# A scan with a mixture-of-experts FFN behind it: FFN work handed over into the next block, and the clip moved to the front of a step

## What is computed

```python
def _derivative(q, p, drive, coupling, bias):
    i_couple = jnp.tanh(q) @ coupling.T
    dq = q - q ** 3 / 3.0 - p + drive + i_couple + bias
    dp = EPSILON * (q + ALPHA - BETA * p)
    return (dq, dp)
# one step of time: four evaluations of it (Runge-Kutta), then
q_next = jnp.clip(q_next, -CLAMP, CLAMP); p_next = jnp.clip(p_next, -CLAMP, CLAMP)
...
# the FFN, on all 2048 states q
logits = x @ W_router.T
rw, sel = jax.lax.top_k(softmax(logits), 2);  combine[token, sel] = rw
shared_out = (silu_and_mul(x @ Ws_gate_up) @ Ws_down) * sigmoid(x @ W_sgate.T)
gu = jnp.einsum('th,ehi->eti', x, We_gate_up);  h = silu_and_mul(gu)
sparse_out = jnp.einsum('eth,te->th', jnp.einsum('eti,eih->eth', h, We_down), combine)
return shared_out + sparse_out
```

## Time and profile before

| | us |
|---|---|
| median of 3 runs | 743.61 |
| the 3 runs | 742.8, 743.61, 743.67 |
| profiled execution | 745.0 |
| its span, first to last instruction | 743.1 |
| PE, DVE, ACT, POOL busy | 679.2, 671.2, 431.0, 174.6 |

### The profile page before, as it was taken

The page is one execution under the profiler, slowest core; times in us unless marked ns, Lnnn a source line. Parts: engine busy times, 40 slices in busy tenths (PEclk is TensorE's granted clock), DMA queues, the critical chain, the costliest instruction groups (busy, mean ns, idle before and its releaser), DMA issues.

```text
span 743.1 us, 33477 instructions
## 1 busy us (share of the span) xinstructions
PE 679.2 (91%) x12101; PEld 601.7 (81%) x12101; DVE 671.2 (90%) x4624; ACT 431.0 (58%) x2310; POOL 174.6 (23%) x372
## 2 busy tenths in 40 slices
PE   2437999999999999999999999999999999999998
PEld 1326888888888888888888888888888989888888
DVE  5899999999999999999999999999999899999972
ACT  3865646556565655656565565656556565654643
POOL 0001221312222231222223122221312213132233
PEclk9999999999999999999999999999999999999999
DMA  8600000000000000000000000000000000000000
GB/s 319 189 2 2 3 3 11 4 9 4 10 3 3 11 3 10 4 10 4 3 11 3 11 2 11 2 4 10 4 10 4 10 4 2 11 4 10 4 9 9
DMA packets 8630, 13.64 MB, mean 18 GB/s; under 512 B 1520, under 2 KB 7984, under 8 KB 8208
## 3 DMA queue, kind: packets, MB, share of 16 engines
q1 hardware_dynamic: 8464, 11.50, 4.5%
HBM read 9.40 MB, written 2.10 MB: 15 GB/s over the span
## 4 chain that ended last, share of the span: by engine, by line
PE 62%; DVE 22%; issue 7%; ACT 3%; POOL 3%; DMA 2%; SPq 0%; DVEq 0%; POOLq 0%; ACTq 0%
PE up_ps L507 18%; PE down_ps L521 14%; PE coup_ps L456 12%; PE coup_ps L449 11%; PE warm_ps L537 5%; DVE th_lo L685 2%; POOL hidden L839 2%; PE route_ps L488 2%; DMA wf<-in_w_up 2%; DVE q L720 2%; DVE p_part L623 2%; DVE q_raw L720 1%; DVE w L618 1%; DVE p_sum L643 1%; DVE force L707 1%
## 5 line engine op out<-in xcount | busy, mean ns | idle before, releaser
L507 PE MATMUL up_ps<-q_hi,w 128*128 128x128 f16 x2176 | 226.5, 220 | 0.7 <-POOL q_lo L809 0.7
L449 PE MATMUL coup_ps<-th_hi,c 128*128 128x16 f16 x4096 | 183.2, 171 | 30.1 <-ACT th_hi L348 27.8
L449 PEld LDWEIGHTS coup_ps<-th_hi,c 128*128 128x128 f16 x4096 | 148.0, 97 | 71.3 <-ACT th_hi L348 48.0
L348 ACT ACTIVATE th_hi<-q 128x32 f16<-128x32 f32 x384 | 88.0, 229 | 189.0 <-DVE q L720 187.3
L507 PE MATMUL up_ps<-q_lo,w 128*128 128x128 f16 x1088 | 197.2, 220 | 0.0
L839 POOL TENSOR_TENSOR hidden<-hidden,comb_s 128x128 f32<-128x128 f32 x272 | 124.5, 459 | 295.4 <-PE coup_ps L456 274.4
L507 PEld LDWEIGHTS up_ps<-q_hi,w 128*128 128x128 f16 x2176 | 175.0, 98 | 0.8 <-POOL q_lo L809 0.8
L521 PE MATMUL down_ps<-hidden,wd 128*128 128x128 f32 x1088 | 157.8, 285 | 0.0
L456 PE MATMUL coup_ps<-th_lo,c 128*128 128x16 f16 x2048 | 132.2, 173 | 24.3 <-DVE th_lo L685 17.1
L521 PEld LDWEIGHTS down_ps<-hidden,wd 128*128 128x128 f32 x1088 | 133.3, 191 | 0.0
L456 PEld LDWEIGHTS coup_ps<-th_lo,c 128*128 128x128 f16 x2048 | 85.8, 97 | 58.5 <-DVE th_lo L685 32.5
(11 more groups left out here) (87 smaller groups left out, 910.0 us busy)
## 6 DMA issues: line engine op xcount, KB each, us to landing
wf<-in_w_up SPq DMA_DIRECT2D x1, 4224.0 KB, 13.5
wd<-in_w_down SPq DMA_DIRECT2D x1, 2048.0 KB, 22.4
out<-out_s SPq DMA_DIRECT2D x16, 128.0 KB, 2.1
xs<-in_x SPq DMA_DIRECT2D x1, 1920.0 KB, 19.0
sel<-in_spread SPq DMA_DIRECT2D x1, 408.0 KB, 18.8
cf<-in_coupling SPq DMA_DIRECT2D x1, 256.0 KB, 2.4
xs<-in_x SPq DMA_DIRECT2D x1, 128.0 KB, 2.2
ident<-in_identity SPq DMA_DIRECT2D x1, 64.0 KB, 2.3
```

The costliest lines, as they stand in the source:

```text
L348: nc.scalar.activation(th_hi[:], q[:], ACT.Tanh).then_inc(hi_ready, 1)
L449: nc.tensor.matmul(coup_ps[:, m * B:(m + 1) * B], c16[:, part, k, m * P:(m + 1) * P], th_hi[:, k, :], start=part == m == k == 0, stop=Fals ...
L507: last = nc.tensor.matmul(up_ps[j % 4][:, h * TOK:(h + 1) * TOK], w16[:, part, k, h, j * P:(j + 1) * P], q[:, k, :], start=n == 0, stop=n ...
```

## The change

1. **Two blocks of FFN at a time.** The FFN's stages now run from 0 to 43. In stage st of block b the engines do stage st + 32 of block b-2 and stage st of block b-1 (`ffn_stages`). PE takes the newer block first (`[::-1]`), the others the older. The tail is 44 stages long, with the end of block 14 and all of block 15.
2. **New lists.** The hides stand in stages 5, 10, 13 to 31, never where k is 0; a product tile two stages ahead of its hide. Spreads move to 15, 19, 23, 27, 31. Weighs stand in 16 to 30 and 34 to 41, never where k is 3. Eight of 17 down tiles fall into the next block's stages 1 to 10, and PE has no stage any more with two down tiles and a spread.
3. **Router steps one by one.** The seven steps stand in stages 1, 2, 3, 6, 7, 8, 9 instead of two in stage 1 and one each in 2, 4, 5, 6, 7, and share no stage with a hide. The power goes from stage 2 to 3, `comb` from 7, 8, 9 to 10, 11, 12, the turn from 10 to 13.
4. **Final sum.** One instruction of 128x256 in stage 43 (stage 11 of the block two later), instead of two of 128x128 in stages 2 and 3.
5. **`q_lo`** is made in two halves of 128x128, in stages 0 and 1.
6. **The clip first.** Where k is 0, DVE clips q before it makes `rest` for that evaluation, not behind it. The `rest` of the second evaluation goes from the end of the k = 0 stage (behind `force`) to the front of the k = 1 stage, and `base3` and `base4` there go one place back each, behind `cubic` and behind `force`.
7. **Unread matmuls.** `WARM` follows the new lists: 5, 0, 5, 1, 5, 13, 13, 0, 1, 5, 5 in stages 0 to 10 (before: 6, 10, 11, 1, 1, 1, 13, 1, 1, 1, 13), 78 in a block (before: 83).

```diff
-UP_AT = [st for st in range(3, 25) if st % 4 != 2]
-SILU_AT = [s + 1 for s in UP_AT]
-HIDE_AT = [s + 2 for s in UP_AT]
-SPREAD_AT = [12, 15, 18, 22, 26]
+HIDE_AT = [5, 10, 13, 14, 15, 17, 18, 19, 21, 22, 23, 25, 26, 27, 29, 30, 31]
+SILU_AT = [s - 1 for s in HIDE_AT]
+UP_AT = [s - 2 for s in HIDE_AT]
+TURN_AT = 13
+SPREAD_AT = [15, 19, 23, 27, 31]
 COPY_AT = [SPREAD_AT[j // GROUP] + 1 + (j % GROUP) // 2 for j in range(TILES)]
-WEIGH_AT = list(range(13, 30))
-DOWN_AT = [14, 18, 18, 22, 22, 25, 26, 26, 27, 27, 28, 28, 29, 29, 30, 30, 31]
+WEIGH_AT = [16, 17, 18, 20, 21, 22, 24, 25, 26, 28, 29, 30, 34, 37, 38, 40, 41]
+DOWN_AT = [18, 18, 22, 22, 26, 26, 30, 30, 31, 33, 33, 34, 36, 39, 39, 41, 42]
+FINISH_AT = STAGES + 11
 assert len(UP_AT) == len(DOWN_AT) == len(WEIGH_AT) == TILES and len(SPREAD_AT) == GROUPS
 assert all(w >= max(s, c) and d > w for w, s, c, d in zip(WEIGH_AT, HIDE_AT, COPY_AT, DOWN_AT))
-
-WARM = [6, 10, 11] + [max(0, 13 - 12 * UP_AT.count(st) - 8 * DOWN_AT.count(st) - 4 * SPREAD_AT.count(st))
-                      for st in range(3, STAGES)]
+assert DOWN_AT[-1] < FINISH_AT < STAGES + DOWN_AT[0]
+
+WARM = [max(0, 13 - 12 * UP_AT.count(st) - 8 * (DOWN_AT + [0]).count(st) - 8 * DOWN_AT.count(st + STAGES)
+            - 4 * SPREAD_AT.count(st)) for st in range(STAGES)]
...
-ROUTE_AT = {1: (0, 1), 2: (2,), 4: (3,), 5: (4,), 6: (5,), 7: (6,)}
-FINISH_AT = [2, 3]
+ROUTE_AT = {1: (0,), 2: (1,), 3: (2,), 6: (3,), 7: (4,), 8: (5,), 9: (6,)}
...
             for b in range(BLOCKS):
-                block_of(b, b - 1 if b else None)
+                block_of(b)
+
+        def ffn_stages(b, st):
+
+            return [(f, at) for f, at in ((b - 2, st + STAGES), (b - 1, st)) if 0 <= f < BLOCKS]
+
+        def tail_stages():
+
+            return [x for st in range(FINISH_AT + 1) for x in ffn_stages(BLOCKS, st)]
...
-            def one_block(b, f):
+            def one_block(b):
                 for st in range(STAGES):
                     couple(b, st)
                     prepare(b * STAGES + st)
-                    if f is not None:
-                        if isinstance(f, int) and st == 0:
-                            pe.wait_ge(in_wd, 2 * 16)
-                            pe.wait_ge(in_const, 4 * 16)
-                        ffn(f, st)
+                    if b == 1 and st == 0:
+                        pe.wait_ge(in_wd, 2 * 16)
+                        pe.wait_ge(in_const, 4 * 16)
+                    for f, at in ffn_stages(b, st)[::-1]:
+                        ffn(f, at)
+                    if b:
                         for _ in range(WARM[st]):
                             nc.tensor.matmul(warm_ps[:, 0:P], c16[:, 0, 0, 0:P], c16[:, 0, 0, 0:P],
                                              start=True, stop=True)
 
...
 
                     if t:
-                        dve.wait_ge(p_clipped, t)
+                        dve.wait_ge(q_ready, n)
+                        if i == 1 and b:
+                            dve.wait_ge(q_split, (KC + 1) * b)
+                        nc.vector.tensor_scalar(q, q_raw[:], CLAMP, -CLAMP, ALU.min, ALU.max).then_inc(q_clipped, 1)
                     nc.vector.tensor_tensor(rest[0][:], drive[:, t, 0], p_now[:], ALU.subtract
                                             ).then_inc(rest1_ready, 1)
-                    if t:
-                        dve.wait_ge(q_ready, n)
-                        if i == 1 and b:
-                            dve.wait_ge(q_split, 2 * b)
-                        nc.vector.tensor_scalar(q, q_raw[:], CLAMP, -CLAMP, ALU.min, ALU.max).then_inc(q_clipped, 1)
                 prepare(n)
                 slot()
                 if k == 0:
@@ -666,10 +675,10 @@
                 else:
                     dve.wait_ge(q_ready, n)
                 if k == 1:
+
+                    nc.vector.scalar_tensor_tensor(rest[1][:], q0_of(i), R2_Q1, base[:, 0, :].rearrange(
+                        "p (m b) -> p m b", m=KC), ALU.mult, ALU.add).then_inc(rested, 1)
                     update_p()
-
-                    nc.vector.tensor_tensor(base3[:].rearrange("p m b -> p (m b)"), base[:, 1, :],
-                                            q0_of(i), ALU.add).then_inc(based_q, 1)
                 elif k == 2:
 
                     nc.vector.scalar_tensor_tensor(rest[2][:], q_in[1][:], R3_Q2, base3[:], ALU.mult, ALU.add
@@ -691,8 +700,8 @@
                     update_p()
                 elif k == 1:
 
-                    nc.vector.scalar_tensor_tensor(base4[:], q0_of(i), R4_Q1, base[:, 2, :].rearrange(
-                        "p (m b) -> p m b", m=KC), ALU.mult, ALU.add).then_inc(based_q, 1)
+                    nc.vector.tensor_tensor(base3[:].rearrange("p m b -> p (m b)"), base[:, 1, :],
+                                            q0_of(i), ALU.add).then_inc(based_q, 1)
                 elif k == 2:
 
                     nc.vector.scalar_tensor_tensor(base42[:], q_in[1][:], R4_Q2, base4[:], ALU.mult, ALU.add
@@ -705,11 +714,10 @@
 
                 dve.wait_ge(cubed, n + 1)
                 nc.vector.tensor_tensor(force[:], rest[k][:], cubic[:], ALU.subtract).then_inc(forced, 1)
-                if k == 0:
-
-                    dve.wait_ge(based, t + 1)
-                    nc.vector.scalar_tensor_tensor(rest[1][:], q, R2_Q1, base[:, 0, :].rearrange(
-                        "p (m b) -> p m b", m=KC), ALU.mult, ALU.add).then_inc(rested, 1)
+                if k == 1:
+
+                    nc.vector.scalar_tensor_tensor(base4[:], q0_of(i), R4_Q1, base[:, 2, :].rearrange(
+                        "p (m b) -> p m b", m=KC), ALU.mult, ALU.add).then_inc(based_q, 1)
                 elif k == 3 and t + 1 < T:
 
                     dve.wait_ge(p_clipped, t + 1)
@@ -755,16 +763,15 @@
                                                      prob[:, rank:rank + 1], ALU.is_equal, ALU.mult)
                 op.then_inc(routed, 1)
 
-            def finish_chunk(f, m):
-
+            def finish(f):
 
                 dve.wait_ge(down_ready, TILES * (f + 1))
-                if not (isinstance(f, int) and f == 0):
+                if f:
                     dve.wait_ge(stored, 16 * f)
                 nc.vector.tensor_tensor(
-                    out_s[:, m, :].rearrange("p (t b) -> p t b", t=STEPS),
-                    down_ps[:, m * TOK:(m + 1) * TOK].rearrange("p (t b) -> p t b", t=STEPS),
-                    xs[:, bass.ts(f, STEPS), m, :], ALU.add).then_inc(out_ready, 1)
+                    out_s[:].rearrange("p m (t b) -> p m t b", t=STEPS),
+                    down_ps[:, 0:KC * TOK].rearrange("p (m t b) -> p m t b", m=KC, t=STEPS),
+                    xs[:, bass.ts(f, STEPS)].rearrange("p t m b -> p m t b"), ALU.add).then_inc(out_ready, 1)
 
             def ffn(f, st):
                 for r in ROUTE_AT.get(st, ()):
...
-                if f and st in FINISH_AT:
-                    finish_chunk(f - 1, FINISH_AT.index(st))
-
-            def one_block(b, f):
+                if st == FINISH_AT:
+                    finish(f)
...
+                if st < KC:
+
+                    pool.wait_ge(q_split, (KC + 1) * f + 1)
+                    nc.gpsimd.tensor_tensor(q_lo[:, st], q_trace[:, st].rearrange("p t b -> p (t b)"), q_hi[:, st],
                                             ALU.subtract).then_inc(q_split, 1)
-                if st == 2:
```

More of the change, by code:

```diff
@@ L540, in _ @@
             blocks(one_block)
-            for st in range(STAGES):
-                ffn(BLOCKS - 1, st)
+            for f, at in tail_stages():
+                ffn(f, at)
         @block.vector
@@ L780, in ffn, with one_block @@
                                                        ).then_inc(hidden_ready, 1)
[L781 to L784 removed]
+                if st == FINISH_AT:
+                    finish(f)
+            def one_block(b):
                 for st in range(STAGES):
                     def slot(st=st):
[L787 to L788 removed]
+                        for f, at in ffn_stages(b, st):
+                            ffn(f, at)
                     scan_stage(b, st, slot)
@@ L794, in _ @@
                                     ).then_inc(q_clipped, 1)
-            for st in range(STAGES):
-                ffn(BLOCKS - 1, st)
-            for m in range(KC):
-                finish_chunk(BLOCKS - 1, m)
+            for f, at in tail_stages():
+                ffn(f, at)
         @block.gpsimd
```

40 lines of the change are left out of this document (18 added, 22 removed).

## The result

| | before | changed |
|---|---|---|
| median, us | 743.64 (4 runs) | 734.34 (4 runs) |
| runs, us | 742.8 to 743.74 | 733.84 to 735.21 |
| profiled execution; its span | 745.0; 743.1 | 735.21; 733.4 |

The ratio is 0.9879, interval 0.9862 to 0.9896: 9.3 us faster. The forecast was 722.2 with a range from 716 to 731. The sign was right, and more than half of the gain did not come.

What follows compares the result with a forecast made beforehand. The chain tanh, `th_lo`, coupling, next q was taken to bound each stage at 1.29 us. Fourteen blocks -22.8, block 1 -1.1 and tail +2.5 gave -21.4, so 722.2 us, range 716 to 731.

Steps and rivals of the forecast that it cites:

- Lists of weighs and hides: New weigh places: 0.44 us less per block; `p_sum` waiting for a weigh's end, 0.14 into its stage, costs nothing.
- POOL holds first and second: Rival, stage 9: `first` waits for stage 8's weigh, stage grows 0.25 us; 727.8 in all, chance 0.20.
- Block 1: First block with FFN: same relief but no final sum, clock may rise later; 1.1 us less, bounds 0 and 2.
- Clip first: k = 0 stages: `rest` no longer ahead of the clip; 0.04 us less in each of eight, 0.3 per block.
- rival of longer k = 1 stages: Rival: `base4` behind `force` delays L720 by 0.1 us in each k = 1 stage; 735 in all, chance 0.05.
- Down tiles spread out: Stages 19 and 23: no stage with two down tiles and a spread ahead of them; 0.36 us less per block.
- router steps in stages 1 to 7: Router steps alone in their slots: 0.20 us in place of all the excess of stages 1, 4, 5 and 7.
- weighs off `p_part`: Stages 16, 20, 24, 28: no weigh meets the second `p_part`; 0.11 us less each, 0.44 per block.
- Final sum: Stage 11: the single sum waits for the last down passes and adds 0.32 us, bounds 0.2 and 0.45.
- Tail: End of the kernel: more product tiles behind a later turn; 2.5 us more, bounds 1.5 and 4.5.
- Small holds: Anywhere in a block, such as the hold behind a first weigh: 0.1 us allowed per block.

Runs made afterwards that it cites:

- x2_one_wait: Changed kernel, but POOL waits for `coupled` once per stage and only in stages where it has work; 726.15 us.
- x11_q_lo_whole: Kernel of `x2_one_wait` with `q_lo` made by one 128x256 instruction in stage 0, as before the change; 728.41 us.
- x3: Changed kernel with the weigh of tile 15 (stage 8 of the next block) over 8 of its 128 columns; 732.46 us.
- x4: Changed kernel with block 1's unread matmuls filled up for the down tiles that block does not have yet; 733.68 us.
- x9: Changed kernel with one POOL wait for `coupled` per stage, in every stage, also those without work; 727.7 us.

## Why the prediction was wrong, point by point

- *Lists of weighs and hides, "cost nothing; bounds 0 and 0.1".* This step failed. It took a weigh's end, 0.14 into the next stage, from a trace in which POOL had a weigh in every stage from 13 to 29 and passed one `coupled` wait for each, and carried it over to a program that passes two per stage and has stages without a weigh. The diff of POOL's loop shows the added wait; I priced POOL's instructions and not its waits. `x2_one_wait` is 8.2 us faster, and its blocks are 0.57 shorter, 0.57 x 14 = 8.0: stage 17 0.16, stages 21, 25, 29 0.055 each, stage 9 0.23, together 0.56.
- *Rival "POOL holds first and second", 0.25.* It is what happened in stage 9, with 0.23. I gave it 0.20 and took the other value in the sum. That its price came out is luck. It was worked out for a weigh that ends 0.14 into stage 9. In `x2_one_wait` the weigh ends just there (369.39 + 0.46 = 369.85) and `first` keeps its 0.28, which ends at 369.88 anyway: a held row begins on time and ends with the weigh, and does not begin behind it. The 0.23 came because the weigh ended 0.38 into the stage.
- *Block 1, "1.1 less, bounds 0 and 2".* It took 0.47 more: 6.8 us at 1.2 GHz, out of bounds. I had the mechanism and thought of one or two product tiles, and not that the clock, once risen, falls back. Beside stage 9, six stages of the block take 1.7 us: 4, 6 and 7 before the clock rises at 74.2, and 12, 13 and 14 in the stretch shown and at its end. Without that, in `x2_one_wait`'s trace, the block is 1.7 less than before, inside the bounds.
- *Clip first, 0.04 in eight stages.* Right in six. Stages 0 and 8 stay at 1.34. In stage 8 the router's `which_f` now stands in the slot, which I priced at nothing; `th_lo` begins 0.44 into it and 0.38 into stage 12. In stage 0 the clip begins 0.07 into the stage and in stages 8 to 28 0.015, and only there does the vector engine pass a wait of its own for `driven` just ahead of it, so it may be this engine's waits that cost here; that was not tried. The rival of longer k = 1 stages has no part in it: `x2_one_wait` has them at 1.29.
- *Down tiles spread out, 0.36; router steps in stages 1 to 7; weighs off `p_part`, 0.44.* Right: stages 19, 23, 4, 5, 7 and 16, 20, 24, 28 are all at 1.29. Stage 1, forecast at 1.37, is 1.29: the logits' copy begins 0.10 into it and not 0.14, and its 0.08 did not come. `x11_q_lo_whole` shows what else the prediction missed there: with `q_lo` in one piece the stage is 1.42. For stage 9 the forecast had 0.12 for `first` and `second`; with the weighs early it is 0.08.
- *Final sum 0.32.* Measured 0.33, and its length of 0.41 was 0.42. *Tail +2.5.* From the last `th_hi` (715.47 and 703.20 in the two traces) to the span's end it is 27.7 before and 30.2 now, +2.5. The turn of the changed kernel in the chain that ended last, with the last q clipped at 704.49, is 8.2 after it, forecast 8.0:

```profile
704.49 0.19 DVE q_trace L800
...
712.69 0.06 PE route_ps L487
...
726.26 4.09 PE down_ps L531 x36
```

- *Small holds, 0.1.* Too little. Beside what is named above, single stages in single blocks come out 0.07 to 0.35 long: the sum of each stage's median is 42.39, the mean block 42.65, 0.26 more (before 43.51 and 43.56). In block 5's stage 28 the coupling's last pass ends at 273.79 and `force` at 273.82, and the next q begins at 274.26:

```profile
274.26 0.25 DVE L728 SCALAR_TENSOR_TENSOR q<-coup_ps,c_un,force 128x32 f32<-128x32 f32 x1 [0.44 <-DVE force L716]
```

  Nothing that the profile shows held it. It is no accident of one execution: this pause and fourteen more are in the same stages of the same blocks, with lengths within 0.06, in the six kernels with the changed lists and the new order (the changed one, x2, x3, x4, x9, x11), also where earlier stages had become shorter. They go with a place in the vector engine's instruction stream. Counted from the first row of its trace, waits included, the row that comes late is the 64th or 65th of a run of 128 in 12 of the 16 pauses of blocks 2 to 14, which make 3.2 of their 3.7 us (in the trace before 5 of 6, and 0.8 of 0.9 us). The packets of queue q14, which the page calls "instruction", are of 8192 bytes, which is 64 for each of 128. So the fetching of instructions is a suspect; no run tested it, most places 128 rows apart show no pause (12 of 35 do), and the cause stays open. For small differences this matters: a change of order or of lists moves these pauses too, and they differ by 1 to 3 us in all between the traces here.

The terms add up to the miss of a block: late weighs 0.56, stages 0 and 8 0.10, the pauses 0.16 above what I allowed, the sum 0.01, less 0.08 for stage 1 and 0.04 for `first` and `second`, 0.71 of 0.72.

With the POOL waits mended and nothing else, the forecast's own sum would have been 4 us off (726.15), inside its range.

## What to carry to other kernels

A helper loop that now runs twice per step doubles its waits too. Count them as instructions of that engine, above all in front of work whose end some other engine can run into. And when a row's start time is carried over to a new schedule, ask what stands ahead of it in its own queue there: here 0.24 to 0.35 us of lateness on an engine that is busy 24% of the time cost 8 us. The old trace may show the price already, as stage 14 did here. Work in a slot costs only what ends beyond the slack, so the same instruction is nearly free where its input is old and dear where it waits.
